# Graph attention on one core: steps of 1024 edges with one TensorE signal each, and a scan from both sides

## The reference

```python
h = maximum(layernorm(x), 0)
idx = concatenate([edge_index, edge_index[:, ::-1]])      # 400,000 edges
src, dst = idx[:, 0], idx[:, 1]
gl, gr = (h @ Wl.T)[src], (h @ Wr.T)[dst]                 # 4 heads of 16
score = (att * leaky_relu(gl + gr, 0.2)).sum(-1)          # one per edge and head
m = segment_max(score, src)
ex = exp(score - m[src])
alpha = ex / (segment_sum(ex, src)[src] + 1e-16)
out = segment_sum(gr * alpha, src)
x = x + gelu(concatenate([out, h]) @ W1.T + b1) @ W2.T + b2
```

## Time and profile before

| | us |
|---|---|
| median of three runs | 9896.93 (9879.18 to 9920.47) |
| span of the profiled execution | 10034.3 |
| of it: up to the first gather of the attention | 0 to 1151.5 |
| attention, up to the end of the last chunk's scan | 1151.5 to 7353.8 |
| messages, between the first and the last sum | 7637.3 to 9970.4 |

### The profile page before, as it was taken

The page is one execution under the profiler, slowest core; times in us unless marked ns, Lnnn a source line. Parts: engine busy times, 40 slices in busy tenths (PEclk is TensorE's granted clock), DMA queues, the critical chain, the costliest instruction groups (busy, mean ns, idle before and its releaser), DMA issues. The chain is left out here.

```text
span 10034.3 us, 108018 instructions
## 1 busy us (share of the span) xinstructions
PE 3861.6 (38%) x25399; PEld 3480.9 (35%) x25400; DVE 4726.8 (47%) x10656; ACT 752.2 (7%) x1207; POOL 4978.3 (50%) x4913
## 2 busy tenths in 40 slices
PE   1011123444444444444444444444484333333445
PEld 1011112434343434333343434343472233333443
DVE  8999634454545454545544454445462122222222
ACT  3011101000000000000000000000000000000000
POOL 0000265555454545555565545454504666666664
PEclk9965555555555555555555555555555555555555
DMA  2000011212121212122121212121611111111111
GB/s 20 0 0 0 19 41 41 57 49 59 49 57 49 57 49 58 48 54 54 48 59 50 58 48 58 48 58 48 56 53 40 43 45 44 44 44 42 44 44 33
DMA packets 498404, 444.25 MB, mean 44 GB/s; under 512 B 178490, under 2 KB 394682, under 8 KB 498018
## 3 DMA queue, kind: packets, MB, share of 16 engines
q0 software_dynamic: 156672, 160.75, 9.9%
q1 hardware_dynamic: 340050, 279.02, 9.3%
q10 hardware_dynamic: 1296, 0.22, 0.0%
HBM read 325.70 MB, written 113.85 MB: 44 GB/s over the span
## 5 line engine op out<-in xcount | busy, mean ns | idle before, releaser
L815 POOL DMA_INDIRECT rows<-gr_table,stage x3328 | 3357.3, 1009 | 3730.8 <-DVE stage L998 2756.7
L1329 POOL DMA_INDIRECT message<-h_table,edge_stage x1568 | 1605.4, 1024 | 854.2 <-issue 464.0
L868 PE MATMUL bank<-gl_parts,hot_t 128*128 x10008 | 772.3, 241 | 2781.7 <-ACT hot_t L951 1738.1
L868 PEld LDWEIGHTS bank<-gl_parts,hot_t 128*128 128x128 bf16 x10008 | 680.3, 131 | 2912.2 <-issue 2887.3
L854 PE MATMUL bank<-terms,hot_sum 128*128 128x68 f32 x6656 | 1588.6, 422 | 6.6 <-DVE terms L1027 6.4
L854 PEld LDWEIGHTS bank<-terms,hot_sum 128*128 128x128 f32 x6656 | 1516.2, 333 | 8.7 <-DVE terms L1027 6.3
L1356 PE MATMUL bank<-message,edge_hot 128*128 128x64 f32 x3136 | 720.5, 424 | 1490.0 <-DVE message L1401 1338.8
L1356 PEld LDWEIGHTS bank<-message,edge_hot 128*128 128x128 f32 x3136 | 683.7, 330 | 1526.9 <-DVE message L1401 1371.0
L1011 DVE TENSOR_TENSOR z<-bank,rows 128x256 f32<-128x256 f32 x832 | 349.9, 421 | 1408.3 <-remote 1283.2
L1050 DVE TENSOR_TENSOR acc<-acc,bank 128x68 f32 x832 | 187.2, 225 | 1712.3 <-remote 1529.8
L951 ACT COPY hot_t<-bank 128x512 bf16<-128x512 bf16 x834 | 488.0, 585 | 5311.7 <-remote 4099.8
(11 more groups left out here) (266 smaller groups left out, 3405.4 us busy)
## 6 DMA issues: line engine op xcount, KB each, us to landing
gr_rows<-rows SPq DMA_DIRECT2D x832, 128.0 KB
rows_again<-gr_rows SPq DMA_DIRECT2D x832, 128.0 KB
rows<-gr_table,stage POOLq DMA_INDIRECT x3328
edge<-in_edge_attr SPq DMA_DIRECT2D x195, 256.0 KB
message<-h_table,edge_stage POOLq DMA_INDIRECT x1568
gr_table<-gr SPq DMA_DIRECT2D x1, 1536.0 KB
h_table<-h_sb SPq DMA_DIRECT2D x1, 1536.0 KB
out<-x_sb SPq DMA_DIRECT2D x1, 1536.0 KB
```

The source lines that it names most:

```text
L815: pool.indirect_dma_start(rows[k][:, g, :], None, m.gr_table[:, :], bass.IndirectOffsetOnAxis(stage[k][:, g:g + 1], 0)).then_inc(s_gath[k] ...
L868: last = pe.matmul(bank[2 + slot][:, g * D:(g + 1) * D], hot_t[slot][:, g * P:(g + 1) * P], m.gl_parts[:, bass.ds(blk, 1), part * D:(part ...
L1329: pool.indirect_dma_start(rows[k][:, e, :], None, m.h2_table[:, :], bass.IndirectOffsetOnAxis(stage[k][:, e:e + 1], 0)).then_inc(s_gath[k] ...
```

## The change

A step is now two groups, 1024 edges; gathers have eight slots of a step instead of sixteen of a group. Each engine's iteration handles one step. VectorE makes hot_t itself: SyncE loads the step's 1024 places in one row, spread over all 128 partitions (place_b, bf16, four slots, from a table place_rows that decode now writes to DRAM), and a comparison with each partition's own number gives the matrix already turned. TensorE's transposes and ScalarE's copies are gone. TensorE's iteration is left(q + 2) and then the scatter of r, with one signal, s_step, at the end. VectorE waits for s_step once, at the head of its step, for both z of step q and the sums of step r - 2. Two slots (LAG = 2) hold hot_t, hot_sum, terms and the PSUM results.

In the scan the marks come by DMA, issued by ScalarE, from a table pen_rows that decode writes; the scores are transposed at once into two banks; forward and backward running maxima are both taken from the scores and joined by a maximum at the end, so that all edge values go to one partition in one trip and both initial values come back in one. Only the block of the one node in question is rescaled.

The core of the diff (declarations of tiles and semaphores, and the rest of scan and decode, are left out):

```diff
-GATHER_SLOTS = 16
-PAD = GATHER_SLOTS * GROUP_TILES
+STEP_GROUPS = 2
+STEP_TILES = STEP_GROUPS * GROUP_TILES
+STEP = STEP_TILES * P
+STEPS = GROUPS // STEP_GROUPS
+CHUNK_STEPS = STEPS // CHUNKS
+GATHER_SLOTS = 8
+LAG = 2
...
         @block.sync
+            def load_place(q, slot):
+                at_least(sp, s_hot, q - V + 1)
+                sp.dma_start(place_b[slot][:, :], m.place_rows[bass.ds(q, 1), :].to_broadcast([P, STEP])
+                             ).then_inc(s_place[slot], 16)
...
                     if part.score:
-                        sp.wait_ge(s_gath[k], (j + 1) * 16 * GROUP_TILES)
+                        load_place(q + LAG + 2, (k + LAG + 2) % V)
+                        sp.wait_ge(s_gath[k], (j + 1) * 16 * STEP_TILES)
...
         @block.tensor
+            def left(q, slot):
+                blks = [pe.value_load(m.blk_i[0:1, bass.ds(q * STEP_GROUPS + i, 1)], min_val=0, max_val=BLOCKS - 1)
+                        for i in range(STEP_GROUPS)]
+                pe.wait_ge(s_hot, q + 1)
+                at_least(pe, s_z, q - LAG + 1)
+                for g in range(STEP_TILES):
...
+            def scatter(r, slot):
+                pe.wait_ge(s_terms, r + 1)
+                at_least(pe, s_acc, STEP_GROUPS * (r - LAG + 1))
...
                     if part.score:
-                        turn_hot(q + 2, k % 2)
+                        last = left(q + LAG, k % LAG)
                     if part.sum:
-                        pe.wait_ge(s_terms, r + 1)
...
-                        last.then_inc(s_sum_ps, 1)
-                    if part.score:
-                        left(q + 2, k % 2)
+                        last = scatter(q - CHUNK_STEPS, k % LAG)
+                    last.then_inc(s_step, 1)
...
         @block.scalar
-            def move_hot(q, slot):
-                at_least(act, s_left, q - 1)
-                act.wait_ge(s_hot_ps, q + 1)
-                nc.scalar.copy(hot_t[slot][:, :], bank[slot][:, :].bitcast(BF16)[:, 0:GROUP_TILES * P]
-                               ).then_inc(s_hot_t, 1)
...
         @block.vector
+            def hot_of(q, slot, place_slot, loads):
+                dve.wait_ge(s_place[place_slot], loads)
+                dve.tensor_scalar(hot_t[slot][:, :], place_b[place_slot][:, :], m.iota_node[:, 0:1], None, ALU.is_equal
+                                  ).then_inc(s_hot, 1)
...
+                    dve.wait_ge(s_step, q + 1)
                     if part.score:
-                        dve.wait_ge(s_left, q + 1)
...
+                        hot_of(q + LAG, k % LAG, (k + LAG) % V, place_loads(j, k + LAG))
...
-                        dve.wait_ge(s_hot_ps, q + 1)
-                        hot_of(hot[k % 2], q + 2).then_inc(s_hot, 1)
...
+                    if add:
+                        accumulate(r - LAG, k % LAG, 0)
...
-                    if part.sum and not (first and k == 0):
-                        accumulate(r - 1, (k - 1) % 2)
+                    if add:
+                        accumulate(r - LAG, k % LAG, 1)
...
             def scan(part):
-                chain.link(dve.tensor_tensor_scan(top[:, down], pen_s[:, 1:SCAN + 1][:, down], top_f[:, down], init[:, :],
+                chain.link(dve.tensor_tensor_scan(fore[:, :], pen_s[:, 0:SCAN], score_s[:, :], init[:, 0:1], ALU.add, ALU.max))
+                chain.link(dve.tensor_tensor_scan(top[:, down], pen_s[:, 1:SCAN + 1][:, down], score_s[:, down], init[:, 1:2],
                                                   ALU.add, ALU.max))
+                chain.link(dve.tensor_tensor(top[:, :], top[:, :], fore[:, :], ALU.max))
```

More of the change, by code:

```diff
@@ L817, in _ @@
             body(0)
-            with pool.Fori(1, CHUNKS * steps) as j:
+            with pool.Fori(1, CHUNKS * outer) as j:
                 body(j)
@@ new lines, in scatter @@
+            def scatter(r, slot):
+                pe.wait_ge(s_terms, r + 1)
+                at_least(pe, s_acc, STEP_GROUPS * (r - LAG + 1))
+                for i in range(STEP_GROUPS):
+                    for g in range(i * GROUP_TILES, (i + 1) * GROUP_TILES):
+                        last = pe.matmul(sums_of(slot, i), hot2[slot][:, g, :],
+                                         terms[slot][:, g * HEADS:(g + 1) * HEADS, :].rearrange("p h w -> p (h w)"),
+                                         start=g % GROUP_TILES == 0, stop=g % GROUP_TILES == GROUP_TILES - 1)
+                return last
@@ L899, in scan @@
-                pe.wait_ge(s_score_s, (c + 1) * n_fills)
-                pe.wait_ge(s_pen_s, (c + 1) * n_fills)
-                pe.wait_ge(s_edge, e + 1)
-                for v in range(3):
+                pe.wait_ge(s_sorted, c + 1)
+                if part.sum:
+                    pe.wait_ge(s_acc, c * CHUNK_GROUPS)
+                for g in range(ROW_TILES):
+                    last = pe.transpose(bank[6 + g // HALF][:, g % HALF * P:(g % HALF + 1) * P], top[:, g * P:(g + 1) * P],
+                                        m.ident[:, :])
@@ L933, in _ @@
-            for q in range(2):
-                turn_hot(q, q)
-                left(q, q)
+                    pe.wait_ge(s_inits, c + 1)
+                    pe.matmul(bank[7][:, 2:3 + HEADS], m.ones[0:1, :], again[:, :], start=True, stop=True)
+                else:
+                    pe.wait_ge(s_inits, c + 1)
+                for v in range(2):
+                    last = pe.transpose(bank[7][:, v:v + 1], inits[0:1, v, :], m.ident[0:1, 0:1])
+                last.then_inc(s_inits_ps, 1)
@@ L937, in turn @@
+                pe.wait_ge(s_exp, c + 1)
+                for g in range(ROW_TILES):
+                    last = pe.transpose(bank[6 + g // HALF][:, g % HALF * P:(g % HALF + 1) * P],
+                                        score_s[:, g * P:(g + 1) * P], m.ident[:, :])
+                last.then_inc(s_back_ps, 1)
+            for q in range(LAG):
+                left(q, q).then_inc(s_step, 1)
             def turn(part):
@@ L988, in _ @@
             chain = Chain(dve, s_chain)
[L989 to L995 removed]
+            att = m.att[:, :].unsqueeze(1).to_broadcast([P, STEP_TILES, D])
@@ L1004, in body @@
-                    tile = (U * j + k) * GROUP_TILES - part.c * CHUNK_TILES
+                    q, r = U * j + k, U * j + k - CHUNK_STEPS
+                    add = part.sum and not (first and k < LAG)
+                    tile = q * STEP_TILES - part.c * CHUNK_TILES
                     if not isinstance(tile, int):
-                        tile = nc.s_assert_within(tile, 0, CHUNK_TILES - GROUP_TILES, skip_runtime_bounds_check_because=
-                                                  "a step's groups are its chunk's")
+                        tile = nc.s_assert_within(tile, 0, CHUNK_TILES - STEP_TILES, skip_runtime_bounds_check_because=
+                                                  "a chunk's steps are its tiles")
```

456 lines of the change are left out of this document (195 added, 261 removed).

## The result

The changed kernel takes 9438.51 us (median of four runs, 9428.37 to 9470.61), the kernel before on the same chip 9901.39: a ratio of 0.953, 95% interval 0.950 to 0.956. It is faster by 463 us, where 1,268 were forecast. Its profiled execution lasted as long as the others, 9436.3.

What follows compares the result with a forecast made beforehand. The attention loop was taken as bound by TensorE signals arriving late while GpSimd gathers. Thirteen chunks of 378 us plus 20 make 4934 instead of 6202.3, saving 1,268 from 9896.9: 8,629 us, range 8,100 to 9,650.

Steps and rivals of the forecast that it cites:

- The bound: Attention loop: waits for TensorE's signals, late while GpSimd gathers without a pause; 6.8 us a group, 3.37 where nothing is late.
- VectorE's step: VectorE's own work per attention step of 1024 edges: 5.25 us, hot_t 0.6 of it, against 6.7 before.
- The loop through TensorE: Attention with two slots: two steps take at least 5.25 + 3.84 us plus signal delay; GpSimd's work stays longer up to 12.
- delay D: How late TensorE's signal comes in the attention loop: 4.5 us a step for 0, 7.5 for 6, 10.5 for 12.
- The row of the same shape: Message stage as model for the attention step: 11.96 us, 11.07 without its second matmuls; 11.0 taken.
- The scan: End of each chunk: 38.4 us before, 34 after (28 to 40), 8 of it credited to gathers running meanwhile.
- The sum: Whole attention: chunk 32 x 11.0 + 34 - 8 = 378 us, thirteen plus 20 make 4934 against 6202.3; 1,268 saved.
- C: Rival: signals come through only in GpSimd's pauses, two steps each, 13.6 us a step; 9,010 to 9,812 us; chance 0.22.
- A: The forecast itself: attention steps of 10.4 to 11.9 us, chunks of 358 to 407; 8,370 to 9,010 us; chance 0.47.
- B: Rival: GpSimd is the bound, scan hidden behind gathers, chunks of 325 to 358 us; 7,940 to 8,370 us; chance 0.20.
- D: Rival: one signal passes per GpSimd pause, rows of 8 gathers, 17 us a step; slower, 11,230 us; chance 0.10.
- The rules of the Trainium skill: Attention: increments of 26.3 ns make five fewer signals worth 55 us; hot_t locking out GpSimd costs 146 us at most.

Runs made afterwards that it cites:

- e12: Changed kernel with each attention step's eight indirect gathers replaced by one plain DMA of ScalarE's queue, always the same 1,024 rows: 6435 us, ratio 0.641 to the kernel before.
- e5: The changed kernel itself, unchanged, on a further chip: 8256.81 us against 8205.31 for the kernel before, ratio 1.005.
- e6: The kernel before itself, unchanged, run for its trace on a chip where signals are in time: 8199.83 us.
- e1: Changed kernel with only the first of the eight gathers of each attention step: 6186 us, where the kernel before took 8147.74.
- e7: Changed kernel with left multiplying one of its three parts (8 matmuls a step instead of 24), before at 9891.75: 9241 us, ratio 0.934.
- e2: Changed kernel with left multiplying one of its three parts, on a chip where the kernel before took 8147.74: 8218 us.
- e10: Changed kernel with every matmul of left done twice (48 a step instead of 24), same signals: 9961 us, ratio 0.993 to the kernel before.
- e15: Changed kernel; attention gathers wait for TensorE's signal of the previous step, message gathers for that of two steps back: 9130.47 us, ratio 0.913 to before.
- e16: Changed kernel; GpSimd starts attention step q's gathers only after TensorE's signal of step q - 2: 9140.65 us, ratio 0.914 to the kernel before.
- e11: Changed kernel; GpSimd starts attention step q's gathers only after TensorE's signal of step q - 1: 9088 us, ratio 0.906 to the kernel before.
- e14: Kernel before with one wait more: GpSimd starts group q's gathers only after TensorE's signal of group q - 2: 9394.80 us, ratio 0.938.
- e13: The changed kernel once more, unchanged, on one more chip where the kernel before took 10004.57: 9508.61 us, ratio 0.949.

## Why the prediction was wrong

**The bound** was read rightly: waits for TensorE while GpSimd gathers, three late signals a group. e12 shows that without GpSimd's gathers they are gone, and e5 and e6 that on another chip they are not there at all, which one trace can't tell.

**VectorE's step** was right: forecast 5.25, measured 5.39 in e1, where nothing holds it; hot_t 0.492 us, 0.40 of it until the next instruction starts, against 0.6.

**The loop through TensorE** is the step that failed: 11.0 us a step were forecast, 12.35 measured. I took left and scatter at their durations in rows 4 and let only a delay D of the signal vary, up to 12 us, so that GpSimd's own work was always the longer. Both were mistaken: it is each instruction that is delayed, and so the delay grows with what is queued, 31.3 us in the cycle above and up to 49.5. My own condition for "wrong" (over 12 us late) was met., a signal 41 us late while GpSimd gathered on, already went against D up to 12.

**The row of the same shape** was the wrong neighbour: the messages have one signal per eight gathers too, but 16 matmul records in most steps against 16 + 24. Taking off 0.89 us for the second set of matmuls was mistaken as well: on e6's chip the messages take (8131.6 - 5997.5) / 195 = 10.94 us a step with that set in. What 11.96 had above that goes with a late TensorE: before's page has 768.8 us of waits of agg for "remote", e6 none. Held against a chip with prompt signals, each stretch of 1,024 edges (a step with its share of the scan) loses the more the more records it has. The chunks are read as above, from the last instruction of the scans: e7 (6581.5 - 1615.3) / 12, its like on a prompt chip e2 (5808.8 - 1513.5) / 12, e5 (5802.6 - 1511.6) / 12, e6 (5764.4 - 1518.2) / 12. The chips differ, so small differences count for little.

| | records of matmuls | us longer per 1,024 edges | from |
|---|---|---|---|
| messages of the change | 16, in 48 steps 32 | 0.9 | 11.84 - 10.94 |
| e7, one part | 24 | 1.7 | (413.8 - 357.9) / 32 |
| the change | 40 | 2.4 | (433.0 - 357.6) / 32 |
| e10, left twice | 64 | 3.6 | (471.8 - 357.6) / 32 |
| the kernel before | 48 | 3.8 | (474.5 - 353.9) / 32 |

The last row is out of line: with 48 records and six signals the kernel before loses more than e10 with 64 and one. So the instructions are not all; signals, or the trips that hang on them, cost too. The change has fewer of both, and no run separates what each of them gave it.

**The scan** was forecast at 34, less 8. By itself it was right: from the last z of a chunk to the next z e12 has 39.6 us in the middle chunks, less the step of 5.4: 34. In the changed kernel the same is 53.1 - 5.4 = 48. What was left out is how it begins: VectorE must first add the last two steps' sums, and their signals come out of the slow row. acc has 7 such waits for "remote", 140.1 us in all. The longest:

```profile
5534.64 0.27 PE L883 MATMUL bank<-terms,hot_sum 128*128 128x68 f32 x1 [2.52 <-issue]
5537.45 0.27 PE L883 MATMUL bank<-terms,hot_sum 128*128 128x68 f32 x1 [2.53 <-issue]
...
5533.74 0.94 POOL L821 DMA_INDIRECT rows<-gr_table,stage  x1 [0.30 <-issue]
...
5541.65 1.36 PE L871 MATMUL bank<-gl_parts,hot_t 128*128 x22 [0.49 <-issue]
...
5542.83 0.23 DVE L994 TENSOR_TENSOR acc<-acc,bank 128x68 f32 x1 [24.45 <-remote]
...
5548.23 0.23 DVE L994 TENSOR_TENSOR acc<-acc,bank 128x68 f32 x1 [0.63 <-DVE acc L994]
...
5577.35 0.69 DVE L1007 TENSOR_TENSOR z<-bank,rows 128x512 f32<-128x512 f32 x1 [3.32 <-issue]
```

24.45 us of waiting before the scan, then 5577.35 - 5548.23 = 29.1 for all of it. The 38.4 of before count from the last reduction; from there it is 5577.35 - 5517.99 = 59.4 here.

**The sum.** Twelve chunks at 433.0 instead of 378 are 660 us, the first at 473.5 instead of 398 another 76: 736, and 4934 + 736 = 5670 = 6824.9 - 1155.1. In the terms of the sum a chunk is 32 x 12.35 = 395 for the steps and 38 for the scan, where 352 and 26 stood. The miss in the trace is 9436.3 - 8766 = 670; the other 66 came back outside the attention, 24 in the messages and 45 between the last scan and the messages. The latter says nothing on the change: that stretch takes 233.8 us in e15 and 277.6 in e16, on one chip and with the same instructions in it. The medians fell by 463 and the traces' spans by 598: the profiled execution of before was 137 us above its median, that of the change was not above its own. To carry the difference over unchanged took that for granted.

**The rivals.** C has the size (9,010 to 9,812; measured 9,438) and its cycle of rows and pauses, with four steps to a pause instead of two, but not its reason: signals do come through while GpSimd gathers. That e10 gives its very chunk is luck. A, the forecast, did not happen on these chips. B, GpSimd as the bound with the scan hidden behind gathers, is what e5 is (chunks of 357.6), on a chip where that was true before the change. D did not happen: no run has mostly rows of 8, and e11, with rows of 16 to 24, has steps of 11.5.

**The rules of the Trainium skill.** The 26.3 ns of an increment ("TensorE: Matmul & The Clock Gate", section "The cost: per-tile semaphore tail") could not have shown this: e10 adds 24 matmuls a step, no increment, and costs about 440 us (0.993 - 0.949 of 10,000). That hot_t would hold GpSimd back ("SBUF — State Buffer", section "SBUF: two separate sides") was estimated at 146 us at most; e5 against e6 has 50 us longer gathers in all, and hot_t is not their cause: the 389 gathers that meet it in e5, and neither hot_sum nor terms, take 947 ns, like those beside an idle VectorE (944).

## What to carry to other kernels

A signal that comes late may be a sender that works slowly: look whether the sender's own instructions, where enough of them are queued, stand apart with nothing to wait for, and then count its instructions beside its signals. Where the queue is too short for that, look at the time between two of its signals. When such slowness goes with long rows of work on another engine, a wait that breaks the rows (one line, e14) may be worth more than a new schedule (e13). And a time read on one chip should be held against a second one before a schedule is built on it.

## What the hardware showed unexpectedly

The same kernel takes 8,148 or 8,205 us on two chips and 9,892 to 10,033 on four others (the first comparison's chip, 9,901, may be one of them or a fifth), at much the same mean granted clock (0.53 to 0.54 of full; the one execution of it at 1.0 took 8,131 us on the first of these chips, the others there 8,138 to 8,195). On the slower chips TensorE slows down in a row of gathers. In the changed kernel's first trace, in the row from 3452.28 on, it sends out matmuls at full rate for 9 us (24 in 1.49 us at 3456.25) and, more than 30 us in, one every 1.4 to 2.8 us. After the last gather it takes 3.5 to 7 us until it is at full rate again (last gather over at 3494.31, 17 matmuls in 1.09 us from 3497.82; last gather over at 5534.68, 22 in 1.36 us from 5541.65). VectorE's instructions keep their durations in the same stretch. Why, and why on some chips only, no run here tells.

Gathers that meet terms or hot_sum, f32 instructions of VectorE, take 1.45 and 1.30 us instead of 0.94; those that meet the bf16 comparison hot_t do not get longer (e5).
